# The last block's gate, choice and routing placed in tiles 3 to 6 of the second feed-forward instead of 4 to 10

## What is computed

```python
x = x + 0.5 * _L0_ffn_ref(_layernorm(x, axis=-1), gate_w, expert_bias, w_up, w_down)
x = x + _L0_attn_ref(_layernorm(x, axis=-1), Wq, bq, Wk, bk, Wv, bv, Wo, bo)
x = x + 0.5 * _L0_ffn_ref(_layernorm(x, axis=-1), gate_w, expert_bias, w_up, w_down)
```

```python
logits = jnp.einsum('bsh,eh->bse', x, gate_w) + expert_bias
weights = jax.nn.softmax(logits, axis=-1)
top_w, top_i = jax.lax.top_k(weights, K)
top_w = top_w / (jnp.sum(top_w, axis=-1, keepdims=True) + GATE_EPS)
...
for e in range(E):
    h = jax.nn.gelu(jnp.einsum('bsh,ih->bsi', x, w_up[e]), approximate=False)
    y = jnp.einsum('bsi,hi->bsh', h, w_down[e])
    out = out + sparse_w[..., e:e + 1] * y
...
return out + x
```

## Time and profile before

| | us |
|---|---|
| median of 3 runs | 1253.76 (1251.31 to 1256.22) |
| the profiled execution's own time | 1257.42 |
| its span | 1255.5 |
| TensorE matmuls busy | 928.8 (74%) |
| VectorE busy | 1009.6 (80%) |
| ScalarE busy | 707.3 (56%) |
| POOL busy | 765.9 (61%) |

### The profile page before, as it was taken

The page is one execution under the profiler, slowest core; times in us unless marked ns, Lnnn a source line. Parts: engine busy times, 40 slices in busy tenths (PEclk is TensorE's granted clock), DMA queues, the critical chain, the costliest instruction groups (busy, mean ns, idle before and its releaser), DMA issues.

```text
span 1255.5 us, 32918 instructions
## 1 busy us (share of the span) xinstructions
PE 928.8 (74%) x12872; PEld 752.7 (60%) x12872; DVE 1009.6 (80%) x2109; ACT 707.3 (56%) x1014; POOL 765.9 (61%) x635
## 2 busy tenths in 40 slices
PE   3303988878988878878878988978979778859800
PEld 3302977766766656656656766756766667748700
DVE  7887786987889899899899898898888768538923
ACT  2112766657765755666765776746757646636600
POOL 2178736706867656757656565557987721767264
PEclk9999999989999998999999999988989989969955
DMA  9322424310000000000000000000000012234231
GB/s 336 128 109 73 141 79 111 103 47 6 8 9 8 8 6 8 8 7 8 8 6 2 2 2 2 2 2 19 14 14 13 21 53 72 95 97 122 77 93 50
DMA packets 69508, 61.77 MB, mean 49 GB/s; under 512 B 8304, under 2 KB 60016, under 8 KB 69104
## 3 DMA queue, kind: packets, MB, share of 16 engines
q1 hardware_dynamic: 60448, 42.64, 11.1%
q0 software_dynamic: 8192, 16.79, 4.3%
q10 hardware_dynamic: 720, 0.23, 0.1%
HBM read 30.80 MB, written 28.84 MB: 48 GB/s over the span
## 4 chain that ended last, share of the span: by engine, by line
DVE 30%; POOL 25%; PE 20%; issue 16%; ACT 6%; DMA 2%; DVEq 0%; POOLq 0%; SPq 0%
POOL xs L636 8%; POOL arena_a L1377 5%; DVE arena_b L1275 4%; POOL arena_a L1359 4%; DVE arena_a L1233 3%; PE bank L1043 3%; DVE arena_c L828 3%; ACT arena_c L1153 3%; POOL arena_b L665 2%; DVE arena_c L1271 2%; POOL arena_c L1381 2%; DVE xn_new L426 2%; DVE arena_b L1258 2%; PE bank L742 2%; DVE zt L705 2%
## 5 line engine op out<-in xcount | busy, mean ns | idle before, releaser
L636 POOL DMA_INDIRECT xs<-xhl,slot_idx x128 | 154.1, 1204 | 98.3 <-issue 57.2
L803 ACT ACTIVATE arena_c<-bank,s_pre 128x1024 f32<-128x1024 f32 x92 | 102.3, 1112 | 164.4 <-PE bank L744 158.9
L1377 POOL TENSOR_TENSOR arena_a<-arena_a 128x1024 f16<-128x1024 f32 x64 | 139.4, 2178 | 53.5 <-ACT arena_a L1153 52.9
L1359 POOL TENSOR_TENSOR arena_a<-arena_b,trig_rows 128x512 f32<-128x512 f32 x128 | 160.3, 1272 | 8.6 <-issue 8.6
L1153 ACT ACTIVATE arena_c<-arena_a 128x1024 f16<-128x1024 f32 x64 | 67.6, 1057 | 161.5 <-DVE arena_a L1233 161.5
L757 PE MATMUL bank<-wdn_hi,arena_c 128*128 x736 | 131.2, 222 | 31.8 <-DVE arena_c L828 31.8
L665 POOL DMA_INDIRECT arena_b<-ys,slot_idx x96 | 108.5, 1130 | 66.5 <-DMA ys<-arena_b 38.8
L828 DVE SCALAR_TENSOR_TENSOR arena_c<-arena_c,s_h 128x1024 f16<-128x1024 f32 x92 | 125.2, 1361 | 22.1 <-ACT arena_c L808 22.1
L758 PE MATMUL bank<-wdn_hi,arena_c 128*128 x736 | 131.2, 222 | 0.0
L759 PE MATMUL bank<-wdn_lo,arena_c 128*128 x736 | 131.0, 222 | 0.0
L1258 DVE TENSOR_TENSOR arena_b<-bank,decay 128x512 f32<-128x512 f32 x128 | 82.4, 686 | 41.0 <-PE bank L1043 40.4
(11 more groups left out here) (227 smaller groups left out, 3762.8 us busy)
## 6 DMA issues: line engine op xcount, KB each, us to landing
arena_b<-xs SPq DMA_DIRECT2D x92, 128.0 KB
ys<-arena_b SPq DMA_DIRECT2D x92, 128.0 KB
xs<-arena_c SPq DMA_DIRECT2D x2, 3072.0 KB, 18.2
arena_a<-in_w_up SPq DMA_DIRECT2D x1, 2048.0 KB, 13.0
arena_b<-in_w_down SPq DMA_DIRECT2D x1, 2048.0 KB, 13.6
xs<-xhl,slot_idx POOLq DMA_INDIRECT x128, 2.3
out_x<-x_tok SPq DMA_DIRECT2D x8, 256.0 KB, 2.7
arena_b<-ys,slot_idx POOLq DMA_INDIRECT x96
```

The costliest lines, as they stand in the source:

```text
L636: nc.gpsimd.indirect_dma_start(d["xs"][half], bass.IndirectOffsetOnAxis(slot_idx[:, half, choice, t:t + 1], axis=0), xhl[:, half, t, :], N ...
L1359: i = nc.gpsimd.tensor_tensor(q_trig[h], q_relu[h], trig_rows[:, bass.ds(u * BLK, BLK)], ALU.mult)
L1377: nc.gpsimd.tensor_tensor(q_lo, arena_a[:, 0:2 * BLK], q_hi, ALU.subtract).then_inc(a["q_lo_done"], 1)
```

## The change

The three conditions of each engine get other numbers; the instructions stay as they are. In half 2 of the second feed-forward the gate products go from p = 4 to 3, the exponential from 5 to 4, and on VectorE the split, the logits and piece 0 from 4 to 3. Pieces 1 to 9 stand together at p = 5 instead of in threes at 6, 7 and 8. `route_product` and `route` go from p = 10 to 6.

```diff
--- before.py
+++ after.py
@@ -785,9 +785,9 @@
                     if k and i % 2 == 0:
                         if p == 2:
                             ln_transpose(pe, 1, NBLK - 1)
-                        if p == 4:
+                        if p == 3:
                             gate_product(pe, NBLK - 1)
-                        if p == 10:
+                        if p == 6:
                             pe.wait_ge(gate_read, 2 * NBLK)
                             route_product(pe, 3)
 
@@ -812,7 +812,7 @@
                     if k and i % 2 == 0:
                         if p == 2:
                             ln_copy(act, 1, NBLK - 1)
-                        if p == 5:
+                        if p == 4:
                             gating_exp(act, 3)
 
         def ffn_dve(v, k):
@@ -851,14 +851,14 @@
                             ln_stats(v, 1, NBLK - 1)
                         if p == 1:
                             ln_apply(v, 1, NBLK - 1)
-                        if p == 4:
+                        if p == 3:
                             ln_split(v, NBLK - 1)
                             gate_logits(v, 1, NBLK - 1)
                             gating(v, 3, 0)
-                        if 6 <= p < 9:
-                            for j in range(3 * (p - 6) + 1, 3 * (p - 6) + 4):
+                        if p == 5:
+                            for j in range(1, GATE_PIECES):
                                 gating(v, 3, j)
-                        if p == 10:
+                        if p == 6:
                             route(v, 3)
                     if i % 2 and spread(p, 9):
                         b = (p - 9) // 4
```

## The result

| | before | after |
|---|---|---|
| median of 13 runs each | 1254.57 (1250.01 to 1258.95) | 1248.46 (1243.49 to 1252.69) |
| ratio | | 0.9936 [0.9916, 0.9955] |
| profiled execution, its span | 1257.42, 1255.5 | 1252.19, 1250.3 |
| mean granted clock | 0.929 | 0.930 |

The kernel became 0.64% faster, some 8 us by the ratio; the two medians differ by 6.1. 7.0 were forecast, and 1246.8 us for the median.

A forecast was written before the change was run, and what follows sets the result against it. Bound: the path from routing through 32 scatters, SP's load and the held store to VectorE's `take_y`. First scatter 8.4 us earlier, 7.0 left at the release: 1257.42 - 7.0 = 1250.4, median 1246.8; range 1242.5 to 1251.5.

The forecast's parts named there:

- ScalarE's path to the exponential: ScalarE, tile 4: `h_hi` ends 0.86 us later, at 1032.34; the exponential follows and `low(5)` starts at 1037.6.
- rival (b): Scatters unstretched or clock not falling: 8.4 us gained, up to 1 more if ScalarE is sooner; 1244.4 to 1245.4; chance 0.12.
- The block: VectorE, tile 5: pieces 1 to 9 of the choice run together and take 5.85 us.
- TensorE's wait: TensorE, tile 6: it waits 7.8 us for the mask, from 1037.2 to 1045.0, with nothing hiding it.
- First scatter: POOL: the first scatter comes 6.36 us behind the routing's start, at 1053.1, which is 8.4 us earlier.
- Pace of the scatters: POOL: 31 intervals, 1.47 us each while VectorE works on tiles and 1.26 each while it is idle.
- The tiles' end: First half's tiles end 2.5 us later than before, `low(21)` at 1094.0, with tile 7 counted twice for low clock.
- The release: SP's load goes when the last scatter has landed, at 1100.4 instead of 1107.4: 7.0 us earlier.
- The second half as one piece: The restart, at half clock as before, and the whole second half shift together by 7.0 us.
- (a): VectorE: the routing starts one tile, 2.88 us, later than forecast; gain 4.1 us, time 1249.6; chance 0.20.
- (c): First half becomes the bound, as TensorE stays at the low clock longer after its rest; 1251.9 us; chance 0.05.
- (d): POOL's scatter issues are held by VectorE, 2.27 us each beside tiles; 7.0 us slower, 1260.8; chance 0.03.

The follow-up runs named there:

- the second run: The changed kernel once more, no edit: 1248.29 us against 1257.42 for the kernel before, ratio 0.9941.
- the change with SP's order: Against the change, SP sends the second half's first three loads behind all stores of the first half: 1243.66 us, ratio 0.9928 to the kernel before.
- the kernel of before with SP's order: Against the kernel before, SP sends the second half's first three loads behind all first-half stores, on a slower chip: 1349.58 us, ratio 1.0064.

## Why the prediction was right

By its own steps, behind L434 where nothing else is said:

- *ScalarE's path to the exponential.* `h_hi` of tile 4 was to end at 10.70 and ended at 10.34; `low(5)` was to start at 15.96 and did at 15.60. The gate products cost what was forecast: 3.73 us from `turn_in(5)` to `turn_in(6)` instead of 2.88. The 0.36 is already there at `turn_in(5)`, ahead of everything that was moved, and is a difference between the two executions. Behind `turn_in(5)`, `h_hi` of tile 4 ends at 4.89 and `low(5)` starts at 10.15, both as forecast. So the part of rival (b) that has ScalarE reach the exponential sooner did not come true.
- *The block.* 5.85 us were counted for it; from L516 to the copy behind the mask it takes 1047.63 - 1041.77 = 5.86.
- *TensorE's wait.* 7.8 forecast, 7.80 measured. The reason given, that it waits for the mask, holds only for the instruction at which it shows; with the product elsewhere the block of VectorE makes the same wait.
- *First scatter.* 31.5 forecast, 31.05 measured. Behind `turn_in(5)` it was 25.65 forecast, and 25.60 and 25.63 measured: 8.5 earlier than before, where 8.4 was forecast. In the clock of its own execution the first scatter starts at 1056.02, and the prediction called itself wrong if it started after 1056. 3.3 us of that are the later L434; by the times of the kernel before, in which the prediction reckons, it is 1052.7. The mark should have been set against an instruction ahead of the change.
- *Pace of the scatters.* 1.47 us each beside tile work: 27 intervals from 1056.02 to 1095.86 are 39.84 us, or 1.476. (The prediction's aside, that a pace of 1.435 gives 7.2, is a slip: 42.0 / 1.435 = 29.3 intervals and 1.7 at 1.26 give 7.9. Nothing else rests on it.)
- *The tiles' end.* 2.5 us later were forecast. **This term was mis-sized**: `turn_in(9)` stood at 28.6 where 29.6 was forecast, `turn_in(15)` at 45.9 against 44.3 before, and `take_y(19)` at 69.1 against 67.5: 1.6 later. Counted from `turn_in(5)` it is 1.9, and 1.7 in the second run. Tile 7 at half clock cost less than its length once more: `turn_in(9)` is 23.2 behind `turn_in(5)` where 23.75 was forecast. It weighs little, 0.6 x 0.21 / 1.47 = 0.1 us of the sum.
- *The release.* 7.0 earlier forecast; 7.25 measured behind L434, 6.9 and 7.1 behind `turn_in(5)`; and every link behind it as it was.
- *The second half as one piece.* Here 1.3 us more came: 8.53 at the end against 7.25 at the release. The prediction took the restart for the same in both. It is quicker in the profile after.

TensorE's turn-ins at the restart, before:

```profile
1115.14 0.58 PE L727 MATMUL bank<-ident_h,arena_b 128*128 128x128 f16 x4 [0.53 <-issue]
1116.33 0.59 PE L727 MATMUL bank<-ident_h,arena_b 128*128 128x128 f16 x4 [0.61 <-DVE arena_b L824]
1119.27 0.43 PE L727 MATMUL bank<-ident_h,arena_b 128*128 128x128 f16 x4
```

and after:

```profile
1111.22 0.58 PE L727 MATMUL bank<-ident_h,arena_b 128*128 128x128 f16 x4 [0.54 <-issue]
1112.42 0.38 PE L727 MATMUL bank<-ident_h,arena_b 128*128 128x128 f16 x4 [0.61 <-DVE arena_b L824]
1114.14 0.39 PE L727 MATMUL bank<-ident_h,arena_b 128*128 128x128 f16 x4
```

From the first to the third it is 4.13 us before and 2.92 after, since the second and third run at full clock: the windows say the same.

```profile
1116.00:1119.00 3.00, 2.67 (x15) 2.03 (x16) 0.61 (x2) 0.00 (x0) 0.99 (x1) 0.50 0.44 130
```

(before), and after:

```profile
1112.00:1115.00 3.00, 2.56 (x26) 2.23 (x27) 1.12 (x3) 0.66 (x1) 0.99 (x1) 1.00 0.45 131
```

The shorter wait isn't the reason: in the kernel with the late routing VectorE waited 19.8 us for `ys`, longer than before, and its restart was as quick as the one after (from its first turn-in to the end 138.9 us; 140.4 before, 139.1 after), while the change with SP's order restarted slowly (141.0). Of the eight profiles on undisturbed chips, six need 2.6 to 2.9 us from the first of these turn-ins to the third, both of the change (2.92 and 2.64) among them; the two slow ones are that of before (4.13) and that with SP's order (4.16). The kernel with the late routing and the one without scatters are quick with the same SP order as before. So the slow restart rather belongs to the one profiled execution of before than to its order, but that kernel was profiled only once, and what decides is open. The ratio, 8.0 us with an interval from 5.6 to 10.5, holds both 7.0 and 8.5.

Of the rivals: (a) fell, the routing was at its forecast place. (c) fell on this chip, with the release 8.4 us behind the start of `low(21)`, and came out on the slower ones, through gaps beside the scatters and not through the clock. (d) fell for the scatters: the pace by which they were priced was measured again within 0.4%. The rule of the Trainium skill, "SBUF — State Buffer", section "Who interferes with whom", named beside it is not thereby wrong. The same section puts the making of a DMA's descriptors apart: as an inference, it says that this needs the write side of the shared ports, while a `tensor_tensor` with both inputs in SBUF takes only their read side. So by that section L828 needn't hold a scatter, and (d) was more than the rule says. The rows agree with it to that extent: two scatters and one `low` fit into every 2.87 us, one of the two stretched from 0.96 to about 1.31. For a POOL instruction that computes, the rule holds here: L828 took 6.13 us beside L643's 4.51, where it takes 1.28 alone. The section also says that whoever issues first goes first. The starts in the profile don't sort it so: there L828 starts 0.53 us ahead of L643 and is the one held, while at 159.22 us of the kernel before with SP's order L828 starts 0.52 ahead, keeps its 1.28, and L643 takes 5.15.

This collision needed no experiment to be seen. The profile of before has it in the first feed-forward, where the L643 of the first half runs from 164.61 to 169.13 and the next one follows it:

```profile
165.25 4.96 DVE L828 SCALAR_TENSOR_TENSOR arena_c<-arena_c,s_h 128x1024 f16<-128x1024 f32 x1 [0.23 <-ACT arena_c L808]
...
170.80 4.87 DVE L828 SCALAR_TENSOR_TENSOR arena_c<-arena_c,s_h 128x1024 f16<-128x1024 f32 x1
```

The median, 1248.46, is 1.7 us above the forecast's 1246.8. The forecast was built on a median of 1253.76 for before; that of 13 runs is 1254.57. The rest is within what runs of one kernel differ by.

## What to carry to other kernels

Ask first what a DMA queue stands still for: here one load at the front of SP's queue held a store that had long been ready, and a move far ahead of it could be priced by when that load would go. A block of work put on one engine stops its neighbours for as long as they live on what it copies, wherever their own waits are written; and it pays if what it starts earlier is what ends last. The margin to the other end, here the 8.4 us between the start of `low(21)` and the release, bounds what the next step can gain (6.0 came of it), and it has to be read on the chip the kernel is to run on. Whoever moves a step forward also moves what stands behind it on the same engine: POOL's `add_input` came among the tiles so, and cost up to 4.85 us there. And times of two executions are best counted from the last instruction ahead of the change: from L434 the first scatters of the change's two profiles differ by 0.87 us, from `turn_in(5)` by 0.03.

## What the hardware showed that was not expected

- On two of the chips TensorE stood still beside POOL's indirect DMAs, up to 3.15 us ahead of a single matmul with nothing awaited, 21 to 31 us in all for one set of 32 scatters; in the eight traces from other chips there was no such run of gaps. It is part of a difference of 80 to 92 us in the whole kernel.
- VectorE's L828 lasted 6.13 us beside one POOL TENSOR_TENSOR of 4.51 us, 4.8 times its own 1.28. The same pair stands in all fourteen profiles: wherever L828 was held beside L643, however long, it ended 1.08 or 1.09 us behind the end of that L643.
- Behind its rest at the seam TensorE was back at 2.4 GHz 0.8 us behind its first turn-in in the profile after, and not yet 3.9 us behind it in that before; the length of the wait doesn't sort the kernels.
